# Three products of the first step of a feed-forward layer, issued as six half products by chunk pair

## What is computed

```
q, k, v = split(xn @ W_qkv.T + b_qkv)            # 16 heads of 16
q, k = elu(q) + 1, elu(k) + 1
out = (q @ (k.T @ v)) / clip(q . sum(k), 1e-6)   # linear attention, per head
attn = layernorm(out @ W_proj.T + b_proj) * gamma + beta + xn

h = silu(xn @ w1.T * s1) * (xn @ w2.T * s2)      # 256 -> 1024
h = gelu(h @ h1.T * sh1)                         # 1024 -> 1024
h = gelu(h @ h2.T * sh2)                         # 1024 -> 1024
ffn = h @ w3.T * s3                              # 1024 -> 256
y = x + attn + ffn
```

## Time and profile before

| what | value |
|---|---|
| median of 3 runs | 1523.49 us |
| the profiled execution | 1524.34 us |
| its span, first to last instruction | 1522.5 us |
| TensorE busy (matmul) | 1504.6 us, 99% of the span |
| VectorE, ScalarE, GpSimd busy | 75%, 62%, 31% |
| mean granted clock of TensorE | 0.998 of 2.4 GHz |

### The profile page before, as it was taken

How to read it: one execution, slowest core, us unless ns; L and a number is a source line. 1 busy time by engine, 2 the same in 40 slices (tenths; PEclk the granted TensorE clock), 3 DMA queues, 4 the chain that set the end, 5 groups by cost and what they waited for, 6 DMA issues and landing times.

```text
span 1522.5 us, 33236 instructions
## 1 busy us (share of the span) xinstructions
PE 1504.6 (99%) x11024; PEld 1419.0 (93%) x11024; DVE 1147.9 (75%) x2056; ACT 937.0 (62%) x1727; POOL 469.2 (31%) x555
## 2 busy tenths in 40 slices
PE   9999999999999999999999999999999999999998
PEld 6998999989899998999989999899998989989897
DVE  5747778687787877878678686877868778687786
ACT  4556656566575665756656576565666656566554
POOL 2213415134151332504324052340523415134141
PEclk9999999999999999999999999999999999999999
DMA  8796845737366382754727448184572736637364
GB/s 226 229 313 226 266 136 180 244 101 255 113 218 213 106 270 85 245 186 130 257 88 258 166 142 290 49 262 158 163 262 80 267 121 197 228 102 255 110 215 149
DMA packets 86082, 287.65 MB, mean 189 GB/s; under 512 B 7200, under 2 KB 46240, under 8 KB 62752
## 3 DMA queue, kind: packets, MB, share of 16 engines
q0 software_dynamic: 43296, 231.75, 46.4%
q1 hardware_dynamic: 42048, 54.42, 11.2%
q10 hardware_dynamic: 704, 1.05, 0.2%
HBM read 270.42 MB, written 25.17 MB: 194 GB/s over the span
## 4 chain that ended last, share of the span: by engine, by line
PE 91%; DVE 4%; issue 2%; ACT 2%; POOL 0%; DMA 0%; DVEq 0%; ACTq 0%; POOLq 0%; SPq 0%
PE ps L944 49%; PE ps L919 13%; PE ps L1017 8%; PE ps L822 4%; PE ps L823 4%; PE ps L824 4%; PE ps L966 4%; PE ps L864 2%; DVE values_a L1538 2%; PE ps L885 1%; PE ps L875 1%; PE ps L834 1%; DVE exp_tmp L1518 1%; DVE operands_a L1546 1%; ACT gate_ring L1178 1%
## 5 line engine op out<-in xcount | busy, mean ns | idle before, releaser
L944 PE MATMUL ps<-operands_a,hidden_weights 128*128 128x256 f32 x5040 | 645.9, 282 | 7.0 <-DVE operands_a L1546 7.0
L944 PEld LDWEIGHTS ps<-operands_a,hidden_weights 128*128 128x128 f32 x5040 | 616.0, 189 | 11.2 <-DVE operands_a L1546 10.0
L1579 DVE TENSOR_TENSOR partial_sums<-partial_sums,ps 128x512 f32<-128x512 f32 x300 | 204.6, 686 | 157.2 <-PE ps L944 107.5
L1546 DVE TENSOR_TENSOR operands_a<-values_a,operands_a 128x512 fp32r<-128x512 f32 x315 | 234.2, 763 | 35.8 <-POOL values_a L702 23.9
L710 POOL DMA_DIRECT2D hidden_weights<-weight_blocks x236 | 131.4, 557 | 402.3 <-PE ps L944 383.7
L919 PE MATMUL ps<-xnT,w_ffn 128*128 128x512 f32 x1024 | 253.0, 399 | 0.0
L944 PE MATMUL ps<-operands_b,hidden_weights 128*128 128x256 f32 x1680 | 234.9, 282 | 1.3 <-DVE partial_sums L1579 0.9
L919 PEld LDWEIGHTS ps<-xnT,w_ffn 128*128 128x128 f32 x1024 | 189.0, 188 | 41.9
L944 PEld LDWEIGHTS ps<-operands_b,hidden_weights 128*128 128x128 f32 x1680 | 213.5, 188 | 4.9 <-issue 3.0
L687 POOL TENSOR_TENSOR values_a<-values_a 128x512 f32<-128x512 f32 x30 | 38.3, 1276 | 344.9 <-DVE values_a L1538 344.9
L1243 ACT ACTIVATE values_out<-partial_sums,vectors 128x256 f32<-128x256 f32 x180 | 81.6, 502 | 94.9 <-DVE partial_sums L1579 94.9
(11 more groups left out here) (128 smaller groups left out, 2242.8 us busy)
## 6 DMA issues: line engine op xcount, KB each, us to landing
hidden_weights<-weight_blocks POOLq DMA_DIRECT2D x180, 1024.0 KB, 5.1
hidden_weights<-weight_blocks POOLq DMA_DIRECT2D x60, 512.0 KB, 4.0
raw_weights<-weight_blocks SPq DMA_DIRECT2D x48, 304.0 KB, 2.8
hidden_weights<-in_w_ffn POOLq DMA_DIRECT2D x16, 512.0 KB, 8.0
weight_blocks<-weight_sums SPq DMA_DIRECT2D x16, 512.0 KB, 4.1
weight_blocks<-in_w_ffn SPq DMA_DIRECT2D x16, 512.0 KB, 10.6
out_dram<-acc SPq DMA_DIRECT2D x32, 256.0 KB, 2.2
x<-in_H SPq DMA_DIRECT2D x15, 512.0 KB, 5.5
```

What stands on the lines that cost most here:

```text
L944: r = mm(bank[:, m * HT:(m + 1) * HT], ring_weights[:, place, 2 * g + j, m * P:(m + 1) * P], as_used(buf[:, j, slot[block_of_b], part, :]) ...
L1546: v.tensor_tensor(lo_part(group, block), value(group, block), hi_part(group, block).bitcast(F32), ALU.subtract).then_inc(lo_half.sem, 1)
L1579: v.tensor_tensor(scratch[:, dst, :], scratch[:, kept, :], product_bank(s, i), ALU.add).then_inc(add.sem, 1)
```

## The change

The order of the 48 matmuls of products 1, 5 and 6 of step 0: instead of 1 (G0, G1), 5 (G0, G1), 6 (G0, G1), TensorE issues 1 G0, 5 G0, 6 G0, 1 G1, 5 G1, 6 G1. On ScalarE, `keep_first(t, 0)` moves behind three hi parts. All other orders stay, on VectorE and GpSimd too. All other steps call `product`, which is the two halves in turn.

```diff
-                def product(t, s, i):
+                def half_product(t, s, i, g):
                     block_of_b = X_OF[i]
-                    groups = ("G0", "G1") if s < 2 else ("H0", "H1")
+                    group = (("G0", "G1") if s < 2 else ("H0", "H1"))[g]
...
-                    pe.wait_ge(*product_bank_read(t, s, i))
                     place = ring_place(i)
-                    loaded = (exact_loaded if full else ring_loaded)[PART_OF[i]]
-                    pe.wait_ge(loaded.sem, loaded.at(t, s))
-                    for g, group in enumerate(groups):
-                        buf, slot = operands(group)
-                        for part in range(2):
...
+                    if g == 0:
+                        pe.wait_ge(*product_bank_read(t, s, i))
+                        loaded = (exact_loaded if full else ring_loaded)[PART_OF[i]]
+                        pe.wait_ge(loaded.sem, loaded.at(t, s))
+                    buf, slot = operands(group)
+                    for part in range(2):
...
+                    return r
+
+                def product(t, s, i):
+                    half_product(t, s, i, 0)
+                    half_product(t, s, i, 1).then_inc(prod.sem, 1)
...
-                    product(t, 0, 1)
-                    product(t, 0, 5)
-                    product(t, 0, 6)
+
+                    half_product(t, 0, 1, 0)
+                    half_product(t, 0, 5, 0)
+                    half_product(t, 0, 6, 0)
+                    half_product(t, 0, 1, 1).then_inc(prod.sem, 1)
+                    half_product(t, 0, 5, 1).then_inc(prod.sem, 1)
+                    half_product(t, 0, 6, 1).then_inc(prod.sem, 1)
                     to_rows(t, 0)
...
                 hi_of_difference(t, "G1", "T1")
-                keep_first(t, 0)
                 hi_of_difference(t, "G0", "T4")
                 hi_of_difference(t, "G0", "T3")
                 hi_of_difference(t, "G1", "T2")
+                keep_first(t, 0)
                 hi_of_difference(t, "G1", "T3")
```

More of the change, by code:

```diff
@@ L949, in product @@
-                    r.then_inc(prod.sem, 1)
+                    if g == 0:
[4 more added lines that the diff above has]
+                    for part in range(2):
+                        if s % 2 == 0 and part == 0:
+                            pe.wait_ge(*hi_made(t, group, block_of_b))
+                        elif s % 2 == 0:
+                            pe.wait_ge(*lo_made(t, group, block_of_b))
+                        for m in range(2):
+                            for j in range(2):
+                                begins = m == 0 and g == 0 and part == 0 and j == 0
+                                ends = m == 1 and g == 1 and part == 1 and j == 1
+                                r = mm(bank[:, m * HT:(m + 1) * HT],
+                                       ring_weights[:, place, 2 * g + j, m * P:(m + 1) * P],
+                                       as_used(buf[:, j, slot[block_of_b], part, :]),
+                                       start=i in firsts and begins, stop=i in lasts and ends,
+                                       skip_group_check=True)
```

## The result

The changed kernel takes 1541.32 us (median of 4 runs, 1540.67 to 1541.83), the kernel before 1523.41 in the same comparison: a ratio of 1.0116, interval 1.0104 to 1.0129. The forecast was 1538.7 us, range 1523 to 1545.

The account below looks back on a forecast made before the run. TensorE, busy 1504.6 of 1522.5 us, was taken to bound the kernel, so only its gaps count. 14 x 1.21 - 1.70 = +15.2 us gave 1539.6 us, or 1538.7 us against the median; range 1523 to 1545 us.

Parts of the forecast that it names:

- The old wait: TensorE's wait for lo G1T1 in tile 2 would be gone, with 0.36 us to spare.
- The refill and t3: GpSimd's refill would start 0.85 us after product 1's later end; t3 G1 would start at 238.20, not 236.71.
- The collision: GpSimd's t3 G1 would hold up VectorE's lo G1T2 to 240.04; TensorE idle from 238.22 to 240.08; chance 0.40.
- the two readings: Whether GpSimd's t3 G1 or VectorE's lo G1T2 gets in first: 1538.7 us or 1529.8 us.
- The other reading: Rival: VectorE's lo G1T2 gets in first, lo G0T3 ends late; +0.61 us a tile, 1529.8 us, chance 0.27.
- The rule of who is first: Whichever of VectorE and GpSimd issues first holds the shared port pair; read with recorded starts, 1529.8 us.
- The price: In tile 2 product 7 starts at 241.67, not 240.46: +1.21 us, counted for 14 tiles.
- The last tile: Product 7 starts at 1454.22 in the last tile: -1.70 us, if the clock stays at 2.4 GHz.
- The clock: Rival: TensorE's clock falls to 1.2 GHz behind the 1.86 us waits; +15 to +40 us, chance 0.08.
- ScalarE's part: `keep_first` and hi G1T3 come later, covered by ScalarE's 1.97 us of idle time before 249.06.
- the gain of 0.18 us a tile: Product 6 ends at 239.16, not 239.34, if nothing else moves; VectorE's order sets the gain.

Follow-up runs that it names:

- e4: The changed kernel with t3 G1 computing only the first 8 of 256 columns of each half, leaving work out; 1519.34 us, ratio 0.9967 to the kernel before.
- e1: The changed kernel with GpSimd's first refill of step 0 moved behind t3 G1; 1535.64 us, ratio 1.0073 to the kernel before.
- e7: The kernel before with only ScalarE's move of `keep_first`; 1523.9 us, ratio 0.9998 to the kernel before.
- e5: The changed kernel with VectorE's lo G1T2 ahead of `swap`; 1556.9 us, ratio 1.0213 to the kernel before.
- e3: The changed kernel with ScalarE's `keep_first` back at its old place; 1541.95 us, ratio 1.0114 to the kernel before.
- e2: The changed kernel with product 1 issued whole first, then 5 G0, 6 G0, 5 G1, 6 G1; 1521.59 us, ratio 0.9982 to the kernel before.
- e6: e2 with VectorE's lo G1T2 ahead of `swap` and GpSimd's t3 G1 waiting for lo G1T2; 1519.87 us, ratio 0.9979 to the kernel before.
- e10: e5 with one wait more, GpSimd's t4 G1 waiting for lo G0T3; 1527.48 us, ratio 1.0022 to the kernel before.

## Why the prediction was right

- **The old wait.** Gone, as worked out; 44 loads in a row in every tile from 1 on.
- **The refill and t3.** Forecast at 5.19 us after product 1's first load, measured 5.27: the refill started 0.89 us behind product 1 and not 0.85. e4 and e1 show that this delay matters only through what t3 G1 then meets.
- **The collision.** lo G1T2 forecast to end at 7.03 us, measured 7.11 (241.29 - 234.18); the wait 1.86, measured 1.88. The rows of the last tile before had decided between the two readings, rightly in 13 of tiles 1 to 14 and in the last. The other reading came true in tile 5, at its forecast price (8.00 against 8.06). Some luck was in it: the choice rested on one row of each kind (a lead of 0.39 us lost, 0.48 won), and the lead came out as 0.34 us in tile 2, not 0.23, with 0.46 in tile 5 enough to go the other way.
- **The rule of who is first.** Read with the recorded starts, what the Trainium skill says ("SBUF — State Buffer", Who interferes with whom) would have given 1529.8 us; 1541.32 was measured, and of tiles 1 to 14 only tile 5 went that way.
- **The price.** +1.21 us a tile forecast, +1.33 measured in 13 tiles (94.6 against 93.27) and +0.59 in tile 5: 13 x 1.33 + 0.59 = 17.9 us from tile 1's product 1 to the last tile's, where 16.9 was forecast. The missing 0.12 is about the later t3 (0.08) and 0.03 by which tile 2, from which I took the clock, is slower than the tiles behind it.
- **The last tile.** Product 7 came 1.61 us sooner (forecast 1.70), without the drop of the clock. But that drop isn't the old order's own: in e7 the same idle time (2.18 us) passed without it, so some 1.33 us of the gain is there only against executions in which the clock fell. And about 1.0 us was given back in step 1 at a late refill, which no step of the prediction had; it spoke of the first refill alone. From product 1's first load to the end the tile gained 0.6 us. So 17.9 - 0.6, less 0.2 at the start, is the 17.1 us by which the span grew; in the medians 17.9.
- **The clock.** It stayed at 2.4 GHz behind 14 waits of 1.9 us. e5 shows that the risk was not far: it fell in 7 of 14 tiles behind idle times of 2.2 us.
- **ScalarE's part.** Costed at nothing; e3 and e7 agree.

## What to carry to other kernels

When an interleaving delays the completion of one product, look up who waits for that completion and what stands behind it in that engine's order: here the product's own operands were no trouble, a weight refill on GpSimd was, through the difference queued behind it. Where VectorE works on two SBUF operands (`swap`, with one, was not held up) and GpSimd on SBUF too, a move of some tenths of a microsecond on either can put two such instructions in series, as here; place them against each other by hand, or with a wait, and check the one that the collision would move to. Interleave so that what others wait for is still complete first, as e2 does: it kept the gain of 0.18 us a tile without the cost.

## What the runs showed of the hardware

- **Recorded starts don't say who gets in first.** In tiles 1 to 15 of the kernel before, the changed one, e2 and e7, a lo meets t3 G1 that comes right behind a refill's issue. Recorded 0.29 to 0.42 us ahead of t3 G1, VectorE's lo was held up all the same (17 tiles); recorded 0.46 to 0.52 us ahead, it went in (43 tiles). Without a refill in front, ahead of t4 G1, which waits for a lo, 0.15 to 0.22 us was enough (15 tiles before, 14 after). Whether it is the refill in front that makes the difference was not tested by itself.
- **A waiting lo isn't always next.** In e5 a lo that waited through t3 G1 was kept out by t4 G1 too (2.63 us). In tile 5 of the changed kernel, and in e6, a lo that waited for t3 G1 went in ahead of t4 G1 (1.76 and 0.85 us, t4 1.71 and 1.72). What decides between these stays open; e10 only takes the case away.
- **TensorE's clock.** Idle times of 1.9 us (after, 14 tiles) left it at 2.4 GHz. Behind idle times of 2.0 to 2.3 us it fell to 1.2 GHz in the last tile before and in 7 of tiles 1 to 14 of e5, there at about 1.5 us each; it stayed in e5's other 8 and in e7's last tile (2.18 us), and behind 2.9 us in e2's. So the length of the idle time alone doesn't decide; what does stays open.
